# Exponentials of a state scan in two PSUM banks, B and C by turns in one bank, and the weighing of gathered rows in three instructions

## The reference

```
# layers 0, 2, 3
xp     = x @ w_in + b_in
h      = gelu(batch_norm(depthwise_conv3x3(x)))
offset = h @ w_off + b_off                    # 4 groups x 9 points x (x, y) a pixel
mask   = softmax(h @ w_msk + b_msk, over the 9 points)
y      = sum over points of mask * bilinear(xp at point + offset)    # four corners a sample
x      = x + gamma1 * LN(y @ w_out + b_out)
x      = x + gamma2 * LN(gelu(x @ w_fc1 + b_fc1) @ w_fc2 + b_fc2)
# layer 1: 4 directions, 256 channels, 16 states, 3136 steps a direction
dt, B, C = projections of silu(depthwise_conv3x3(in_proj(LN(x))));  dt = softplus(dt + bias)
h_t = h_(t-1) * exp(dt_t * A) + (dt_t * u_t) * B_t
y_t = sum over the 16 states of h_t * C_t
x   = x + out_proj(LN(sum of directions) * silu(z));  x = x + MLP(LN(x))
```

## Time and profile before

| | |
|---|---|
| median of 3 runs | 31776.09 us |
| the profiled execution's own time | 31708.39 us |
| its span | 31706.4 us |
| POOL busy (gathers alone) | 24065.5 us |
| DVE busy | 22436.1 us |
| PE busy | 23142.6 us |
| ACT busy | 12011.1 us |
| mean granted clock of PE, share of full speed | 0.834 |

### The profile page before, as it was taken

How to read it: one execution, slowest core, us unless ns; L and a number is a source line. 1 busy time by engine, 2 the same in 40 slices (tenths; PEclk the granted TensorE clock), 3 DMA queues, 4 the chain that set the end, 5 groups by cost and what they waited for, 6 DMA issues and landing times.

```text
span 31706.4 us, 280317 instructions
## 1 busy us (share of the span) xinstructions
PE 23142.6 (73%) x94224; PEld 14718.8 (46%) x94224; DVE 22436.1 (71%) x31704; ACT 12011.1 (38%) x20358; POOL 24065.7 (76%) x21172
## 2 busy tenths in 40 slices
PE   5577778777787778777877777777877787767444
PEld 4444445444544454444544454444444454435333
DVE  1288877888588868887688858886688858885111
ACT  1144444444344434443444434443444444433000
POOL 6777777777777777777777777777677777667767
PEclk7788888888888888888988888888888888888666
DMA  3212122221221221211222121212222121112221
GB/s 73 73 49 63 51 64 64 56 63 49 71 59 51 62 70 51 62 48 54 71 58 62 49 72 53 58 50 63 56 55 61 50 70 51 49 42 66 62 56 52
DMA packets 2410607, 1854.10 MB, mean 58 GB/s; under 512 B 1686546, under 2 KB 2045508, under 8 KB 2409164
## 3 DMA queue, kind: packets, MB, share of 16 engines
q0 software_dynamic: 677376, 1388.62, 15.7%
q1 hardware_dynamic: 1731788, 447.55, 6.3%
HBM read 1569.35 MB, written 265.21 MB: 58 GB/s over the span
## 4 chain that ended last, share of the span: by engine, by line
POOL 68%; issue 19%; PE 9%; DVE 2%; ACT 1%; DMA 1%; SPq 0%; POOLq 0%; DVEq 0%; ACTq 0%
POOL d_g L730 68%; PE d_pr L1162 2%; PE d_p L1014 2%; PE l_pc L1127 1%; PE d_pr L1049 1%; DVE l_wk L1287 1%; DMA d_xin<-mid 0%; PE d_pr L1216 0%; SPq L629 0%; PE d_pr L1151 0%; DMA mid<-l_xb 0%; PE l_acc L996 0%; PE d_pr L1150 0%; PE l_acc L1119 0%; PE l_pm L1102 0%
## 5 line engine op out<-in xcount | busy, mean ns | idle before, releaser
L730 POOL DMA_INDIRECT d_g<-table,d_idx x21168 | 24065.5, 1137 | 7598.6 <-issue 6427.4
L1014 PE MATMUL d_p<-d_g,c_ident 128*128 128x128 f32 x43200 | 6435.2, 317 | 3171.5 <-DVE d_g L1318 3169.5
L1014 PEld LDWEIGHTS d_p<-d_g,c_ident 128*128 128x128 f32 x43200 | 6233.1, 231 | 4322.7 <-DVE d_g L1318 3235.7
L996 PE MATMUL l_acc<-l_wk,c_ident 128*128 128x448 f32 x14336 | 7229.8, 634 | 456.2 <-DVE l_yx L1276 360.8
L1318 DVE TENSOR_TENSOR d_g<-d_g,d_wt 128x1536 f32<-128x1536 f32 x1776 | 3101.9, 1747 | 4109.0 <-DMA d_g<-table,d_idx 4106.5
L1299 DVE TENSOR_TENSOR l_wk<-l_wk,l_pb 128x896 f32<-128x896 f32 x3584 | 3829.1, 1068 | 1961.8 <-PE l_pb L965 1954.9
L781 ACT ACTIVATE l_pm<-l_wk,l_a 128x448 f32<-128x448 f32 x3584 | 2272.1, 634 | 7709.3 <-DVE l_wk L1287 7703.1
L996 PEld LDWEIGHTS l_acc<-l_wk,c_ident 128*128 128x128 f32 x14336 | 3161.1, 222 | 2514.4 <-issue 2344.2
L1305 DVE TENSOR_TENSOR l_wk<-l_wk,l_pc 128x896 f32<-128x896 f32 x3584 | 3806.7, 1062 | 22.3 <-ACT l_carry L762 14.7
L1287 DVE TENSOR_TENSOR_SCAN l_wk<-l_wk,l_carry 128x448 f32<-128x448 f32 x3072 | 3518.4, 1145 | 0.0
L1287 DVE TENSOR_TENSOR_SCAN l_wk<-l_pm,l_carry,l_wk 128x448 f32<-128x448 f32 x3072 | 3504.8, 1141 | 2.7
(11 more groups left out here) (177 smaller groups left out, 22365.2 us busy)
## 6 DMA issues: line engine op xcount, KB each, us to landing
d_g<-table,d_idx POOLq DMA_INDIRECT x21168
table<-d_pst SPq DMA_DIRECT2D x2376, 64.0 KB
hd<-d_hst SPq DMA_DIRECT2D x168, 224.0 KB
d_htc<-hd SPq DMA_DIRECT2D x144, 256.0 KB
d_xin<-mid SPq DMA_DIRECT2D x112, 224.0 KB
mid<-d_xo SPq DMA_DIRECT2D x192, 128.0 KB
d_xres<-mid SPq DMA_DIRECT2D x192, 128.0 KB, 2.2
d_xin<-in_x SPq DMA_DIRECT2D x56, 224.0 KB
```

Of the source, the lines that this page charges most:

```text
L730: e.indirect_dma_start(out=m.g[Q % SLOTS][:, j, :], out_offset=None, in_=m.table[k % 2], in_offset=bass.IndirectOffsetOnAxis(ap=m.idx[G % ...
L996: ins = e.matmul(m.acc[:, h, 0:448], m.ident[:, :], m.hb[x % 4][:, h, :], start=(n == 0), stop=(n == 15))
L1014: ins = e.matmul(m.p0[:, t % 2 * 128:t % 2 * 128 + 32 * w], m.ident[:, :], m.g[Q % SLOTS][:, w * p:w * p + w, 32 * r:32 * r + 32], start=( ...
```

## The change

- Half 1 of `exp(dt*A)` goes to the PSUM bank `pc`, half 0 stays in `pm`; each has one buffer, so each waits for the scan of its own half one step earlier. On DVE both scans of a step now stand next to each other.
- Rows B and C use the bank `pb` by turns. Row C of a step (`sC`) is spread after DVE has read B of the next step; C is applied at the head of the next tick (`s2`). The sum over states follows one step behind the scan, where it was two.
- `carry` is copied after both exponentials of the next step, where it stood ahead of them.
- A weighing is three instructions of 4 gathers (128 by 512 numbers) each, where it was one of 12.
- The `+ 1` of softplus (L1338, a DVE instruction a piece) becomes an ACT instruction (Identity with a bias of one). The inverse root of a layer norm over channels, Sqrt on ACT and reciprocal on DVE (L1396, one a chunk of 448 pixels), becomes Ln and Exp on ACT.
- The bilinear weights of four tiles are written by one instruction where it was one a tile (L1532).
- The planner may start the first `pr` of the next stage in the last four tiles when the next stage's convolution has reached its second part, where all of the next stage's input, table and convolution had to be done.

```diff
-        for sig in range(-1, NSTEP + 3):
-            tick = [("sB", i, sig - 1)] * (0 <= sig < NSTEP) + [("s", i, sig)]
+        for sig in range(-1, NSTEP + 1):
+            tick = [("s2", i, sig - 1)] * (sig > 0) + [("s", i, sig)]
             j, q = divmod(sig, 16)
             if 0 <= sig < NSTEP:
                 if 2 <= q <= 10 and j + 1 < len(PIECES):
                     tick.append(("h", i, j + 1, q - 2))
                 if j + 2 < 7 and 8 <= q <= 13:
                     tick.append(("c", i, j + 2, (q - 8) // 3, (q - 8) % 3))
+                tick.append(("sC", i, sig))
             out.append((1.0, tick))
+        out.append((0.0, [("s2", i, NSTEP)]))
         if i + 1 < n:
             out.append((0.0, [("need", order.index((0, i + 1)))]))
         out += after_scan(i, n)
...
                 if t >= NT - 4 and k + 1 < len(order) and self.begun_prep <= k:
-                    if not (self.ahead or self.bank or self.loads or self.prep):
+                    if not self.prep and not self.bank and (k + 1, 1) in self.convs:
                         self.start_prep(k + 1, 0)
...
-        if sig == -1:
-            return [("pb", ("B", s + 1))]
-        return [("pc", ("C", s - 1))] if 1 <= sig <= NSTEP else []
-    if kind == "sB":
-        _, i, sig = item
-        return [("pb", ("B", NSTEP * i + sig + 2))] if sig + 2 < NSTEP else []
+        return [("pb", ("B", s + 1))] if sig + 1 < NSTEP else []
+    if kind == "sC":
+        return [("pb", ("C", NSTEP * item[1] + item[2]))]
...
-        self.dA0, self.dA1 = self.pm[:, 0:448], [wk[5][:, 0, :], wk[5][:, 1, :], wk[6][:, 0, :]]
+        self.dA = self.pm[:, 0:448], self.pc[:, 0:448]
...
         if kind == "s":
             _, i, sig = item
             S = NSTEP * i + sig
+            for h in range(2):
+                x = S + 1
...
+                if sig + 1 < NSTEP:
...
+                    else:
+                        e.wait_ge(s["sh"], 2 * S + h + 1)
+                    kd, c = PIECES[(sig + 1) // 16]
+                    e.activation(m.dA[h], m.dt[P % 2][:, h, :], ACT.Exp, scale=m.aa[:, kd, h, n:n + 1]).then_inc(s[f"dA{h}"], 1)
+            if 0 <= sig < NSTEP:
+                kd, c = PIECES[sig // 16]
                 end = 0 if kd >= 2 else 447
-                e.wait_ge(s["sh"], 2 * S)
-                e.activation(m.carry[:, :, n], m.hb[(S - 1) % 4][:, :, end], ACT.Copy).then_inc(s["ca"], 1)
-            for q, h in ((0, 1), (1, 1), (0, 0)) if sig == -1 else ((sig + 2, 1), (sig + 1, 0)):
...
-                if h == 0 and x:
-                    e.wait_ge(s["sh"], 2 * x - 1)
-                if h == 1 and x >= 3:
-                    e.wait_ge(s["sh"], 2 * x - 4)
-                e.activation(m.dA0 if h == 0 else m.dA1[x % 3], m.dt[P % 2][:, h, :], ACT.Exp,
-                             scale=m.aa[:, kd, h, n:n + 1]).then_inc(s[f"dA{h}"], 1)
+                e.wait_ge(s["sh"], 2 * S + 2)
+                e.activation(m.carry[:, :, sig % 16], m.hb[S % 4][:, :, end], ACT.Copy).then_inc(s["ca"], 1)
         elif kind == "h":
...
                 e.activation(m.e[:, :, :], m.e[:, :, :], ACT.Exp, scale=-1.0).then_inc(s["ex"], 1)
+                e.wait_ge(s["ex"], P + 1)
+                if P >= 2:
+                    e.wait_ge(s["d2"], P - 1)
+                e.activation(m.dt[P % 2][:, :, :], m.e[:, :, :], ACT.Identity, bias=m.one[:, :]).then_inc(s["uu"], 1)
             elif st == 6:
...
-                e.activation(m.rv, m.pm[:, 0:448], ACT.Sqrt, bias=m.eps[:, :]).then_inc(s["f_pm"], 1)
+                e.activation(m.rv, m.pm[:, 0:448], ACT.Ln, bias=m.eps[:, :]).then_inc(s["f_pm"], 1)
+                e.wait_ge(s["f_pm"], J.free("gv", q))
+                e.activation(m.rv, m.rv, ACT.Exp, scale=-0.5).then_inc(s["rvd"], 1)
...
     for item in J.plan:
         kind = item[0]
         if kind == "s":
             _, i, sig = item
             S = NSTEP * i + sig
-            if sig == -1:
-                row_of_B(S + 1)
-            if 1 <= sig <= NSTEP:
-                if J.use["C", S - 1]:
-                    e.wait_ge(s["f_pc"], J.use["C", S - 1])
-                spread(S - 1, m.pc, 16).then_inc(s["p_pc"], 1)
-            if 2 <= sig <= NSTEP + 1:
-                x = S - 2
...
@@ -995,10 +991,10 @@
                 for h in range(2):
                     ins = e.matmul(m.acc[:, h, 0:448], m.ident[:, :], m.hb[x % 4][:, h, :], start=(n == 0), stop=(n == 15))
                 ins.then_inc(s["accd"], 1)
-        elif kind == "sB":
-            _, i, sig = item
-            if sig + 2 < NSTEP:
-                row_of_B(NSTEP * i + sig + 2)
+        elif kind == "sC":
+            x = NSTEP * item[1] + item[2]
+            e.wait_ge(s["f_pb"], J.use["C", x])
+            spread(x, m.pb, 16).then_inc(s["p_pb"], 1)
         elif kind == "sum":
             _, k, t, u = item
             Q = NQ * k + 3 * t + u
...
         if kind == "s":
             _, i, sig = item
             S = NSTEP * i + sig
+            if 0 <= sig < NSTEP:
+                kd, c = PIECES[sig // 16]
+                n = sig % 16
+                way = slice(None, None, -1) if kd >= 2 else slice(None)
+                e.wait_ge(s["f_pb"], J.free("B", S))
+                for h in range(2):
+                    e.wait_ge(s[f"dA{h}"], S + 1)
+                    ini = 0.0 if c == (6 if kd >= 2 else 0) else m.carry[:, h, n:n + 1]
+                    if not isinstance(ini, float):
+                        e.wait_ge(s["ca"], S - 15)
+                    e.tensor_tensor_scan(m.hb[S % 4][:, h, way], m.dA[h][:, way], m.hb[S % 4][:, h, way], ini,
+                                         ALU.mult, ALU.add).then_inc(s["sh"], 1)
+            if sig + 1 < NSTEP:
+                x = S + 1
+                P, n = divmod(x, 16)
+                if n == 0:
+                    e.wait_ge(s["d2"], P + 1)
+                if sig == -1:
+                    e.wait_ge(s["p_pc"], J.full("pi2", 7 * i + 6))
+                    for b, v_ in enumerate(both(7 * i + 6)):
+                        e.wait_ge(s[f"xn{b}"], v_)
+                e.wait_ge(s["p_pb"], J.full("B", x))
+                e.tensor_tensor(m.hb[x % 4][:, :, :], m.dtu[P % 2][:, :, :], bc(m.pb[:, 0:448], 1, 2),
+                                ALU.mult).then_inc(s["f_pb"], 1)
+        elif kind == "s2":
+            _, i, sig = item
+            S = NSTEP * i + sig
+            if sig < NSTEP:
+                e.wait_ge(s["p_pb"], J.full("C", S))
+                e.wait_ge(s["ca"], S + 1)
+                e.tensor_tensor(m.hb[S % 4][:, :, :], m.hb[S % 4][:, :, :], bc(m.pb[:, 0:448], 1, 2),
+                                ALU.mult).then_inc(s["f_pb"], 1)
+            if sig >= 16 and sig % 16 == 0:
                 j = sig // 16 - 1
                 P = 28 * i + j
                 kd, c = PIECES[j]
...
-                    e.wait_ge(s[f"dA{h}"], S + 1)
-                    dA = m.dA0 if h == 0 else m.dA1[S % 3]
-                    ini = 0.0 if c == (6 if kd >= 2 else 0) else m.carry[:, h, n:n + 1]
-                    e.tensor_tensor_scan(m.hb[S % 4][:, h, way], dA[:, way], m.hb[S % 4][:, h, way], ini,
-                                         ALU.mult, ALU.add).then_inc(s["sh"], 1)
-                if h == 0 and sig + 1 < NSTEP:
...
-                        for b, v_ in enumerate(both(7 * i + 6)):
-                            e.wait_ge(s[f"xn{b}"], v_)
-                    e.wait_ge(s["p_pb"], J.full("B", x))
-                    e.tensor_tensor(m.hb[x % 4][:, :, :], m.dtu[P % 2][:, :, :], bc(m.pb[:, 0:448], 1, 2),
-                                    ALU.mult).then_inc(s["f_pb"], 1)
-            if 1 <= sig <= NSTEP:
-                x = S - 1
-                e.wait_ge(s["p_pc"], J.full("C", x))
-                e.wait_ge(s["ca"], x + 1)
-                e.tensor_tensor(m.hb[x % 4][:, :, :], m.hb[x % 4][:, :, :], bc(m.pc[:, 0:448], 1, 2),
-                                ALU.mult).then_inc(s["f_pc"], 1)
...
-            g = m.g[Q % SLOTS][:, 0:parts].rearrange("p j (r c) -> p (j r) c", c=32)
-            wt = bc(m.wt[G % 2][:, t % 4, 12 * u:12 * u + parts].rearrange("p j r -> p (j r)"), 2, 32)
-            e.tensor_tensor(g, g, wt, ALU.mult).then_inc(s["weighed"], 1)
+            for j in range(0, parts, 4):
+                g = m.g[Q % SLOTS][:, j:min(j + 4, parts)].rearrange("p j (r c) -> p (j r) c", c=32)
+                wt = bc(m.wt[G % 2][:, t % 4, 12 * u + j:12 * u + min(j + 4, parts)].rearrange("p j r -> p (j r)"), 2, 32)
+                ins = e.tensor_tensor(g, g, wt, ALU.mult)
+            ins.then_inc(s["weighed"], 1)
...
-            elif st == 4:
-                e.wait_ge(s["ex"], P + 1)
-                e.tensor_scalar(dt[:, :, :], m.e[:, :, :], 1.0, None, ALU.add).then_inc(s["uu"], 1)
...
-                e.wait_ge(s["f_pm"], J.free("gv", q))
-                e.reciprocal(m.rv, m.rv).then_inc(s["dv"], 1)
-                dv += 1
-                e.wait_ge(s["dv"], dv)
+                e.wait_ge(s["rvd"], q + 1)
```

(7 more changed lines are left out.)

64 lines of the change are left out of this document (24 added, 40 removed).

## The result

The changed kernel takes 31370.61 us (median of 4 runs, 31336.84 to 31395.82) where the kernel before takes 31773.79: a ratio of 0.9872 [0.9855, 0.9889], 403 us less. The forecast, 30970 us or 0.8 ms less, was twice that gain. The profiled execution's span is 31393.8 us.

What follows compares the result with a forecast made beforehand. In scan stretches DVE's and PE's in-order walk was to bound, beyond POOL's gathers. Eight stretches -0.6 ms, first and last -0.06, stage starts -0.1, short stretches -0.05: together -0.8 ms, 30970 us; range 30500 to 31500, 8 in 10 29900 to 31950.

Steps and rivals of the forecast that it cites:

- w: Time a scan step loses anew to rows B and C, the forecast's one unknown; taken as 0.14 us over 3584 steps.
- Half 1 in PSUM: 3584 scans lose one SBUF operand, so gathers starting under them no longer wait: -1.09 ms for POOL.
- Weighing in three: Gathers may get a turn between thirds of a weighing: -0.3 ms for POOL, halfway between -1.14 and +0.5.
- Waits for C's row: With one bank, PE spreads C only after DVE reads B: 0.47 us at 509 places, 0.24 ms.
- Waits for B's row: Row B may be spread only after the previous C product: +35 us a scan stretch, between -263 and +180.
- Rival A: Rows cost nothing and POOL cashes its saving: -1.5 to -2.3 ms, 29.9 ms said; chance 0.20.
- rival B: PE reaches row B late, as C must be applied first, and DVE stands: slower, such as 32.3 ms; chance 0.15.
- Stage starts: The new planner rule lets the next stage's preparation run earlier, cutting POOL's waits for `d_idx`: -0.1 ms.
- Less on DVE: L1338 goes (-0.14 ms), L1396 goes (-0.17 ms), fewer bilinear weight instructions (-0.1 ms); DVE's work stays within 0.1 ms.
- POOL waits for `d_p`: POOL's waits grow by 0.5 ms or more, since PE's sum is late more often than the gathers.
- C: DVE has to wait for gathers between the thirds of a weighing: +1.6 ms on DVE, 32.6 ms; chance 0.03.
- D: No change: DVE and PE set the stretches' length (w = 0.35) and stage starts bring nothing; chance 0.07.

Runs made afterwards that it cites:

- e4: The changed kernel with half 1 of the exponential in an SBUF tile instead of PSUM, rows and order as changed: 31387.08 us, 0.988 of the kernel before.
- e1: The kernel before with only the weighing in three instructions: 31047.43 us, 0.9771 of the kernel before.
- e2: The changed kernel with the weighing in one instruction again: 31302.0 us, 0.9855 of the kernel before.
- e3: All parts of the change but the scan's; exponential, rows and scan order as in the kernel before: 31041.48 us, 0.9771 of it.
- e9: The changed kernel with C's row in its own bank and half 1 in SBUF, on a slower chip: 1.0268, again 1.0259, of the kernel before.

## Why the prediction was right and wrong

The sign and the bound held: what POOL saves is cashed only where DVE and PE have waits to give. Two terms were mis-sized, on opposite sides, and the larger error was in the row term: the rows cost 0.65 ms more than forecast in the scans, and the waits for gathers gave 0.4 ms more. That the time lies in the stated range is therefore luck in part. The range was made from w between 0.02 and 0.29 us, and w came out at 0.32.

*Half 1 in PSUM, -1.09 ms for POOL.* Held, and more: 1.48 ms by e4. Counted from the changed kernel's records, 2397 gathers start under the scan of half 1, with over 0.15 us of it left, and have a mean of 946 ns; in e4 2475 such gathers have 1366. DVE's scan is no slower from PSUM (1126 ns, and 1128 from SBUF in e4). It was worth nothing in time. The sum did not foresee that: it let both savings together pay for the waits for gathers, with a cap, and left open that one of them alone would be enough.

*Weighing in three, -0.3 ms taken between -1.14 and +0.5.* Too careful: 0.71 ms of POOL's time in e1, 0.69 between e2 and the changed kernel. Of 1234 gathers that start in a third, over 0.13 us before its end, with another right behind, 949 get their turn at its end and the rest go through the next one too. So both patterns of the earlier trace rows are real, three to one; the 1505 gathers that start under a weighing have a median of 1167 ns, where turns were to give 1.2 us. In the order of before it is worth 720 us; in the changed order it costs 69, DVE's longer work without the return. The two terms make 2.17 of POOL's 2.84 ms, and e3 has 0.20 more than e1 from the parts beside; the last 0.46 ms are not taken apart.

*Waits for C's row, 0.47 us at 509 places, 0.24 ms.* **This is the step that failed.** I counted places where nothing stands between the products in DVE's order, and priced DVE's end to PE's row. It measured 1382 us at 1285 places, 1.08 us each: 520 us at 501 places with nothing between the products, and 862 us at 784 with something. The price per place left out what stands on PE between the two rows (the adding, often at half clock, and at 491 places other matmuls too, which hold 838 us), and the count took a place with a short DVE instruction in it as safe. The reasoning by the bank was itself the wrong cause: e9 keeps these waits without it.

*Waits for B's row, +35 us a stretch.* Wrong in sign, small: 1712 us in all after 1955. Rival A had named a reason, the adding that now lies under the B product; no run tests it. Both rows together have 439 us in the stretch shown and 387 on the mean of eight, where 320 to 340 were forecast and over 430 was to mean rival B. In the form with one unknown, w is (1712 + 1382 - 1955) / 3584 = 0.32 us, not 0.14; the formula then gives -1.04 - 0.04 - 0.21 + 1.14 = -0.15 ms, or 31.63 ms, above the range. The measured -0.40 lies 0.25 ms below that: DVE's waits for gathers fell by 1.64 ms, 1.42 of them in the scans, where the formula had capped them at 1.04. It kept 45 us of them a stretch, and 5 were left.

*Stage starts, -0.1 ms.* Worth nothing: waits for `d_idx` stay (847 us after 792) and 750 us for tables come beside them. In e3, which has the rule, POOL waits as long as in e1, where it was 805 us, for something else:

```profile
POOL d_g L733 <- DMA table<-d_pst: 644.4, 3, 275.2
POOL d_g L733 <- DVE d_idx L1518: 170.7, 4, 157.1
```

*Less on DVE*: DVE is busy for 22390 us after 22436, as said. In the scans alone it is busy for 106 us more, where 0.04 ms less was forecast.

*POOL waits for `d_p`, 0.5 ms or more.* 1.76 ms more. *Gathers' mean 1050 to 1080 ns*: 1003.

*The rivals.* A came nearest to POOL's saving (1.5 to 2.3 ms; 2.8 measured), but its premise, rows at no cost, was wrong. B had the mechanism, PE late to a row, though for the wrong row, and w stayed just short of its point of decision. C did not happen: L1318 of 128x512 takes 646 to 768 ns with a median of 686, and I had worked out 682. The Trainium skill (SBUF — State Buffer, "Who interferes with whom") has DVE blocked as well while the other engine holds the port; here no third of a weighing grew by the 0.94 us of a gather. D's w was nearest, 0.35.

## What to carry to other kernels

Take apart a change of several parts before it is kept: here one part alone (e1, 31047 us) beats both kernels on the chip where all three ran, and the part for the scan eats nearly half of its gain. When an engine in order serves another one, count the lead of each handover, which is what stands on the serving engine ahead of it against what the waiting one has left to do, and not the handover's own latency. A saving on an engine with slack pays only up to the waits for it; once those are gone, as in the changed kernel's scans, a further saving changes nothing.
